# Reordering the first 25 microseconds of a gated cross-attention kernel: the bias row loaded first, the lengths on two queues, the pattern of ones during the wait, and pair 2's transposes behind the first scores

## The reference

```python
def _L0_xattn_ref(memory, query, b, seq_len):
    B, S, _ = query.shape
    dh = UNITS // NUM_HEADS                       # 128 // 16
    k_mem, v_mem = jnp.split(memory, 2, axis=2)
    Q = _split_heads(query, NUM_HEADS) * dh ** (-0.5)
    Kh = _split_heads(k_mem, NUM_HEADS)
    Vh = _split_heads(v_mem, NUM_HEADS)
    logits = jnp.einsum('bhqd,bhkd->bhqk', Q, Kh) + b
    valid = (jnp.arange(S)[None, :] < seq_len[:, 0:1]).astype(jnp.float32)
    logits = logits + MASK_VALUE * (1.0 - valid)[:, None, None, :]
    weights = jax.nn.softmax(logits, axis=-1)
    out = jnp.einsum('bhqk,bhkd->bhqd', weights, Vh)
    return out.transpose(0, 2, 1, 3).reshape(B, S, UNITS)
x = x + jnp.tanh(g_xattn[0]) * _L0_xattn_ref(ctx_2048, _layernorm(x, axis=-1), L0_xattn_b, itok_Bx1_68_817)
x = x + jnp.tanh(g_ffn[0]) * _L0_ffn_ref(_layernorm(x, axis=-1), ...)
```

## Time and profile before

| | us |
|---|---|
| median of 3 runs | 277.94 |
| lowest, highest run | 277.12, 278.81 |
| profiled execution: its own time | 278.2 |
| its span in the trace | 276.4 |
| TensorE busy | 245.5 |
| VectorE busy | 214.0 |
| ScalarE busy | 163.0 |
| GpSimd busy | 158.5 |

### The profile page before, as it was taken

The page is one execution under the profiler, slowest core; times in us unless marked ns, Lnnn a source line. Parts: engine busy times, 40 slices in busy tenths (PEclk is TensorE's granted clock), DMA queues, the critical chain, the costliest instruction groups (busy, mean ns, idle before and its releaser), DMA issues.

```text
span 276.4 us, 8038 instructions
## 1 busy us (share of the span) xinstructions
PE 245.5 (89%) x2966; PEld 184.3 (67%) x2966; DVE 214.0 (77%) x623; ACT 163.0 (59%) x319; POOL 158.5 (57%) x306
## 2 busy tenths in 40 slices
PE   0368979899998999989999979999999999999895
PEld 0135556566665566656567658888888989897865
DVE  4778786899999999997949999858585858585432
ACT  5778785889897989896877642333334242323220
POOL 6888676687877786686892447090919250505120
PEclk9999999999999999999999999999999999999999
DMA  4749997736776866640000000101010101001011
GB/s 110 202 124 209 208 222 181 206 83 196 178 215 160 215 160 162 149 71 6 8 6 2 4 0 0 39 2 38 0 40 0 42 0 30 10 7 31 2 38 38
DMA packets 48461, 23.46 MB, mean 85 GB/s; under 512 B 7680, under 2 KB 48296, under 8 KB 48424
## 3 DMA queue, kind: packets, MB, share of 16 engines
q1 hardware_dynamic: 47520, 22.77, 34.5%
q10 hardware_dynamic: 904, 0.19, 0.4%
HBM read 7.29 MB, written 2.10 MB: 34 GB/s over the span
## 4 chain that ended last, share of the span: by engine, by line
PE 57%; DVE 24%; POOL 5%; ACT 5%; issue 5%; DMA 2%; ACTq 1%; POOLq 0%
PE bank L1102 21%; DVE negmax L1313 11%; PE bank_max L1137 10%; PE bank L1012 7%; PE bank L1044 5%; PE bank L1079 2%; DVE rest L1264 2%; PE bank L1055 2%; PE bank L1095 2%; PE bank L1018 2%; DMA b_rows<-in_L_xattn_b_dram 2%; DVE hsum L1440 2%; ACT stack L760 2%; DVE KV L1326 1%; PE bank L1068 1%
## 5 line engine op out<-in xcount | busy, mean ns | idle before, releaser
L1313 DVE TENSOR_REDUCE negmax<-bank 128x4 f32<-128x512 f32 x128 | 83.3, 680 | 10.7 <-PE bank L1012 10.6
L809 ACT ACTIVATE probs<-bank 128x512 f32<-128x512 f32 x128 | 71.7, 602 | 15.0 <-PE bank L1018 13.9
L1012 PE MATMUL bank<-stack 64*128 64x128 bf16 x512 | 51.9, 235 | 9.6 <-DVE negmax L1313 6.0
L1012 PEld LDWEIGHTS bank<-stack 64*128 64x128 bf16 x512 | 31.7, 101 | 31.2 <-DVE negmax L1313 19.8
L1102 PE MATMUL bank<-u_part,b_part 128*128 128x512 f32 x192 | 52.0, 399 | 0.1
L849 ACT ACTIVATE h<-bank,bi_col 128x512 f32<-128x512 f32 x32 | 22.1, 690 | 49.4 <-PE bank L1102 49.4
L1018 PE MATMUL bank<-stack 64*128 64x128 bf16 x512 | 48.5, 223 | 0.3
L1440 DVE SCALAR_TENSOR_TENSOR hsum<-bank,nbi_col,h 128x512 f32<-128x512 f32 x32 | 23.9, 748 | 24.0 <-PE bank L1102 24.0
L648 POOL TENSOR_TENSOR x_part<-KV,x_part 128x512 fp32r<-128x512 f32 x8 | 10.4, 1301 | 55.8 <-ACT x_part L831 55.8
L1044 PE MATMUL bank<-probs,vpad 128*32 128x128 f32 x1024 | 42.1, 283 | 0.0
L1102 PEld LDWEIGHTS bank<-u_part,b_part 128*128 128x128 f32 x192 | 35.5, 189 | 8.3 <-ACT h L849 0.5
(11 more groups left out here) (136 smaller groups left out, 407.0 us busy)
## 6 DMA issues: line engine op xcount, KB each, us to landing
stack<-part SPq DMA_DIRECT2D x96, 128.0 KB, 3.0
KV<-in_ctx_dram SPq DMA_DIRECT2D x5, 512.0 KB, 4.1
X<-in_x_dram SPq DMA_DIRECT2D x7, 256.0 KB, 4.3
out_dram<-res SPq DMA_DIRECT2D x7, 256.0 KB, 2.3
KV<-in_ctx_dram SPq DMA_DIRECT2D x5, 256.0 KB, 5.6
stack<-bias_line SPq DMA_DIRECT2D x7, 48.0 KB
stack<-max_rows SPq DMA_DIRECT2D x13, 24.0 KB
X<-in_x_dram SPq DMA_DIRECT2D x2, 128.0 KB, 2.4
```

Source lines behind the costliest of these rows:

```text
L809: act.activation(probs[:, i % 4, :], sc2[i % 2][:, :], ACT.Exp).then_inc(s_exp, 1)
L1012: mm = pe.matmul(sc1[i % 2][:, j * 128:(j + 1) * 128], stack[at, s, h0 + 2 * j, q0:q0 + 128], stack[at, s, h0 + 2 * j, 512 + q0:640 + q0], ...
L1313: dve.tensor_reduce(negmax[:, p % 2, n % 2, 8 * (u // 2) + u % 2:8 * (u // 2) + u % 2 + 7:2], bank_cols(sc1[i % 2]), AX.X, ALU.max, negate ...
```

## The change

- ScalarE's queue issues `b_rows` first, then one of the three copies of the lengths, then `seq_row`. The other two copies of the lengths are issued by SP, between K(0) and X(1).
- GpSimd: the addition of `b_rows` is taken out of `bias_sum` into `bias_add`, and stands behind `bias_places`.
- The bias row of slot 0 is put into the stack by ScalarE's queue, behind `copy_line(0)`, and no longer by SP.
- TensorE: bias line 2 is made ahead of the loop and no longer at (0, 0, 2); the transposes of pair 2 stand behind the first quarter of scores. ScalarE copies bias line 2 ahead of `load_gates`.
- VectorE: `first_rest(0)` ahead of `moments_of(1)`, `third_part(0)` ahead of `scale(1)`, the four `stats_of` together.

```diff
-        LINE_AT = {(0, 0, 2): 2, (0, 1, 2): 3, (1, 0, 1): 4, (1, 1, 0): 5, (1, 1, 3): 6, (2, 0, 1): 7}
+        LINE_AT = {(0, 1, 2): 3, (1, 0, 1): 4, (1, 1, 0): 5, (1, 1, 3): 6, (2, 0, 1): 7}
...
             load_x(0)
             load_k(0)
+            for i in range(1, PARTS):
+                sp.dma_start(seq_col[B * i:B * (i + 1), :], seq_len).then_inc(s_col, 16)
             load_x(1)
...
             pair_to_stack(0, 1)
-            bias_to_stack(sp, 0)
             pair_to_stack(0, 2)
...
+
+            def bias_add():
+
                 pool.wait_ge(s_bias, 1)
                 pool.wait_ge(s_b, 16)
                 pool.tensor_tensor(bias_rows[:, :], mask_rows[:, :], b_rows[:, :], ALU.add).then_inc(s_bias, 1)
...
             power(0)
             bias_sum()
             bias_places()
+            bias_add()
             bias_split()
             power(1)
...
-            for i in range(PARTS):
-                act.dma_start(seq_col[B * i:B * (i + 1), :], seq_len).then_inc(s_col, 16)
+            act.dma_start(b_rows[:, :], b.rearrange("(o k) -> o k", o=1).to_broadcast([PARTS * B, S])).then_inc(s_b, 16)
+            act.dma_start(seq_col[0:B, :], seq_len).then_inc(s_col, 16)
             act.dma_start(seq_row[:, :], seq_len.rearrange("b o -> o b").to_broadcast([128, B])).then_inc(s_seq, 16)
-            act.dma_start(b_rows[:, :], b.rearrange("(o k) -> o k", o=1).to_broadcast([PARTS * B, S])).then_inc(s_b, 16)
...
             second_part(0)
             copy_line(0)
+            bias_to_stack(act, 0)
             normalise_first(1)
...
             bias_to_stack(act, 1)
+            copy_line(2)
             load_gates()
...
             place_bias(1)
-            transpose_k(2)
-            transpose_q(2)
+            place_bias(2)
...
                         scores(m, n, c)
+                        if (q, i, c) == (0, 0, 0):
+                            transpose_k(LEAD)
+                            transpose_q(LEAD)
...
+            first_rest(0)
             moments_of(1)
-            first_rest(0)
+            third_part(0)
             scale(1)
-            for n in range(4, 6):
-                stats_of(n)
-            third_part(0)
-            for n in range(6, 8):
+            for n in range(4, 8):
                 stats_of(n)
```

## The result

The changed kernel takes **279.89 us** (median of 5 runs, 279.71 to 281.04) against 277.94. The ratio is 1.0077, with a 95% interval of 1.0051 to 1.0102. It is slower by 0.8%, where I had forecast 277.2 and a range up to 278.6. Its profiled execution took 279.74 us, with a span of 277.9 against 276.4.

A forecast was written before the change was run, and what follows sets the result against it. TensorE, busy 89%, bounds the kernel, so only an earlier loop start helps: 0.5 us from the bias path plus 0.1 to 0.3 from VectorE and the moved line, 277.94 - 0.7 = 277.2 us, range 275.9 to 278.6.

The forecast's parts named there:

- The bound and the pass-through: TensorE, busy 89%, and its feeding work bound the loop; a shift of the mark reaches the end in full.
- the mark: Start of the scores of pair 2, iteration q = 1, at 25.96 us before; forecast near 25.2.
- The wait of 1.44 us goes whatever the load costs within 1.8 us: GpSimd's wait for b_rows vanishes, as b_rows lands at 5.8 and is needed only at about 7.6.
- the sum at the mark: 0.5 from the bias path plus 0.1 to 0.3 from VectorE and the moved line: 0.7 us earlier, bounds 0.1 and 1.3.
- rival (a): Loading b_rows early delays X(0) by x, moving the mark by x - 0.7; chance 0.12 no measurable difference, 0.05 slower.
- Its reader on GpSimd is the mask ... so this too is covered: Third length, issued half a microsecond later at 2.24, costs nothing because the mask stands behind power(0), over at 5.36.
- ScalarE's issue: Slot 0's bias DMA behind copy_line(0) takes 0.9 us of GpSimd's 1.4 gain, leaving 0.5 (0.1 to 0.7).
- VectorE's order: first_rest(0) and moments_of(1) reordered, statistics regrouped: same instructions, covered by VectorE's wait before 11.78.
- The ports: GpSimd's pattern of ones meets VectorE's third slot copy on shared ports: 0.58 us, which power(0) may shed.
- Early scores worth nothing: First scores start at about 15 instead of 17.91, counted at nothing because VectorE isn't ready to read them.
- Line 2 worth something: copy_line(2) ahead of load_gates takes 0.5 us off the path to the mark if it hides there.
- Rival (c): TensorE's step from 1.2 to 2.4 GHz shifts relative to the loop: about 0.5 us either way; chance 0.05.

The follow-up runs named there:

- `other_rows_first`: The changed kernel with b_rows read from 96 different rows of x instead of 96 reads of b; mark 26.82, no time given.
- `vector_order_as_before`: The changed kernel with the loads' issue order, slot 0's bias issue on SP and VectorE's order all as in the kernel before; ratio 0.9981.
- `no_repeated_reads`: `other_rows_first` with seq_row also read from 128 different rows of x; mark 27.05, no time given.
- `only_ones_in_wait`: The kernel before with only GpSimd's addition of b_rows put behind the pattern of ones; 277.40 us against 278.52, ratio 0.9961.
- `loads_as_before`: The changed kernel with the head of both load queues (lengths, seq_row, b_rows) as in the kernel before; ratio 1.0048.

## Why the prediction was wrong, point by point

**The bound and the pass-through** were right within the scatter. The stretch from the start of normalise_first(1) to the mark is 13.44 us in the kernel before and 13.11 in the changed one. From the mark to the end of the span it is 250.4 and 249.7. The mark moved by 2.23, the profiled span by 1.5 and the median by 1.95.

**"The wait of 1.44 us goes whatever the load costs within 1.8 us"** was right, and not the point. I priced the load of b_rows by who waits for it, and not by whom it holds up: the sum at the mark has no term for X(0). I did write that down as rival (a) and gave it 0.17, and my own sign against the sum, X(0) landing after 3.7, came true. The delay came as x = 1.71 (4.78 against 3.07), and b_rows' place at the front is worth 0.93 at the mark. The clue was in the earlier trace rows, where the rate falls from 226 to 92 GB/s while seq_row and b_rows are in flight. I set against it that 48 KB are few and that X(0) was in front. The first is the wrong measure, as `other_rows_first` shows, and X(0) was not in front at all: the two were issued 0.01 us apart on their two queues and landed 4.0 and 3.9 us later.

**"Its reader on GpSimd is the mask ... so this too is covered"** is the step that failed outright. I let the third length land half a microsecond later, because it was issued that much later. It landed at 6.9 instead of about 4, in the stretch that the repeated reads of b_rows and then seq_row had slowed. Nor did I look at what is queued behind the wait on VectorE: the slot copy, the scale and xhat of pair 0. They all came after 6.92, so that the slot copy fell on the mask (1.18 us), and xhat(0) on the pattern (1.51 instead of 0.70). This is worth 0.85, a price that rival (a), x - 0.7, does not hold. By (a) the mark would have come 1.0 later, not 2.23.

**ScalarE's issue** was a term with the wrong size. I took 0.9 us, with the bounds 0.76 and 1.37; it took 1.36 to 1.60 in the six kernels that have it. My reason, that the copy had ended before it, was no reason. In the six, the second DMA of this form on ScalarE's queue, slot 1's, took 0.76 each time; in the kernels where slot 1's is the first one, it took 1.37 or 1.38, as in the earlier trace rows. So the first of these two on that queue is the dear one, wherever it stands. Moving slot 0's there made slot 1's cheaper by 0.6 in exchange (0.76 instead of 1.37). Why the first costs more was not tried. Even my upper bound of 1.37 was too low by 0.2 in three kernels.

**VectorE's order** I costed at nothing, its cover being the wait before 11.78. The wait was there, but what VectorE waited for, power(1), itself waits for the variances that the new order puts behind first_rest(0). The cover was made of the step that was moved. It costs 0.74 at normalise_first(1) and 0.45 at the mark.

**The ports.** I priced one meeting of VectorE and GpSimd at 0.58 us and let it cancel against power(0). The size was right and the count was not: in the changed kernel mask and addition each lost about 0.5 and VectorE's xhat(0) 0.8, while power(0) did shed its part (0.73 instead of 1.29). The Trainium skill (SBUF — State Buffer, Who interferes with whom) has the second engine to ask blocked for the whole instruction, and each stretched step named here lay beside such a step of the other engine. Work that had been apart in time was moved together, both engines having waited for the same length.

**Early scores worth nothing** is supported, though the scores never came as early as I said. I had them at about 15 with pair 0's last product issued at 12.1; it was issued at 14.98 in the changed kernel and the scores began at 18.20, and in `vector_order_as_before` at 14.28 and 16.91. The best case is `no_repeated_reads`, where the first scores began at 16.56 and VectorE read them only at 20.26. Ahead of the third quarter of scores TensorE now waits 1.75 us for VectorE's maximum. **Line 2 worth something** was right in sign: its gain was 0.1 to 0.3 instead of up to 0.5.

**The good part of the sum** was there, but smaller. The whole 1.4 us of GpSimd's wait needs b_rows to be early without holding X(0) up, which no kernel here had with the real b. With b_rows in its old place (`only_ones_in_wait`) the pattern of 1.16 us fits into the wait, the addition takes 0.82 us instead of 0.45, and bias_part and the mark both come 0.78 earlier.

## What to carry to other kernels

A load of one row to many partitions can be dear by the repeated reading of that row and not by its bytes. It belongs behind the loads that the first work waits for, and what does not depend on it goes into the wait, which was the edit here that paid most (0.78 us at the mark). When a transfer is moved, price it by what it will be in flight with, in both directions, and look at everything that stands behind its wait on the engine that reads it. A cover is only a cover if it does not end on the step that was moved.

## What the runs showed of the hardware

- 96 reads of the same 512 bytes, in flight beside two loads of 128 KB, delayed the first of these by 1.7 us (4.0 against 2.3 from issue to landing). 96 reads of different rows of the same size delayed it by 0.3. 128 reads of the same 128 bytes kept a transfer of 0.1 KB on the other queue from landing by another 1.2 us (3.3 against 2.1) and a load of 128 KB behind it by 0.9 (3.1 against 2.2); the rate of all transfers from 4 to 5 us was 71 GB/s with them and 187 without. The Trainium skill (DMA: Bandwidth & Descriptors, Issuing engines are not separate DMA queues) says that the queues of all issuing engines interleave on the same 16 engines. The runs agree: one queue's reads held up the other's.
- The first bias row of the stack on a queue takes its sequencer (the part of an engine that issues) longer than the later ones. In the changed kernel, ScalarE's and SP's timelines, each queue's first and second bias row (ScalarE's first, 1.59 us at 13.44, stands in the chain above):

```profile
19.27 0.76 ACTq L387 DMA_DIRECT2D stack<-bias_line  x1
```

```profile
34.69 0.93 SPq L387 DMA_DIRECT2D stack<-bias_line  x1
...
49.77 0.79 SPq L387 DMA_DIRECT2D stack<-bias_line  x1
```

  The kernel before has 0.93 for the first on SP too, at 12.58, and 0.79 for the next two. On ScalarE the first took 1.36 to 1.60 us. It is not so for every kind of DMA: ScalarE's first issue of the max rows took 0.76 us. What makes the difference was not tried.
- The granted clock of TensorE dipped in some executions, between 160 and 180 us, and with it the time from the mark to the end was 251.1 to 254.8 us in the five profiled executions that had the dip, against 249.0 to 250.5 in the others. It is not tied to the edits: a mean granted clock of 0.994, which all five have, stands at 11 of 25 executions of the kernel before on one chip and at 6 of 21 on another, with medians 1.3 and 1.2 us above the rest. The stretches (columns as in the earlier trace rows) of `loads_as_before`, and below of the changed kernel:

```profile
160.00:170.00 10.00, 8.16 (x49) 6.04 (x48) 9.42 (x37) 3.35 (x6) 4.55 (x4) 0.95 0.01 2
170.00:180.00 10.00, 10.00 (x66) 8.98 (x65) 8.13 (x34) 2.29 (x5) 3.61 (x4) 0.88 0.00 1
```

```profile
160.00:170.00 10.00, 8.16 (x46) 6.54 (x43) 9.55 (x34) 4.03 (x7) 5.74 (x5) 1.00 0.00 0
170.00:180.00 10.00, 9.59 (x65) 8.49 (x64) 8.97 (x40) 3.21 (x7) 2.41 (x4) 1.00 0.10 27
```

  In both, TensorE had been less busy just before (8.16 of 10 us). I read the mean of 0.88 as a part of the stretch at the lower of the two levels, 1.2 instead of 2.4 GHz; why it fell in the one execution and not in the other is open. This scatter is more than half of the whole effect under study, which is why the shares above are read at the mark and not from single times.
- The step from 1.2 to 2.4 GHz near the beginning came 1 to 2 us later in the changed kernel, as the loop did. The weighting of the values took 0.79 us at 46.73 and 0.57 at 48.78, against the earlier trace rows. Rival (c) needed the step to move relative to the loop; it moved with the loop, which came 2.2 later, so the clock's step is no part of the loss.
